# Filter stage of a graph kernel: 252 of 416 groups stored in source-block order and summed by matmuls

## The reference

```
h = relu(layernorm(x))
x = x + segment_sum(h[dst] * (softplus_shifted(edge_attr @ W1 + b1) @ W2 + b2), src)   # filter
h = relu(layernorm(x))
x = x + rgcn(relu(rgcn(h)))       # two relational convolutions, mean per (node, edge type)
```

## Time and profile before

| | us |
|---|---|
| median of 3 runs | 7748.82 (7742.09 to 7757.07) |
| the profiled execution | 7740.94, its span 7739.2 |
| busy: POOL / PE / DVE / ACT | 5938.5 / 4879.2 / 3524.5 / 3186.8 |
| chain that ended last | POOL 19%, all of it `got` at L1321 |
| GB/s moved, mean | 86 |

### The profile page before, as it was taken

One profiled execution on the slowest core, in us unless ns is written; L12 is line 12 of the kernel. 1 busy time (PEld: TensorE's weight loads), 2 busy tenths in 40 slices (PEclk: granted clock), 3 DMA queues, 4 the chain that ended last, 5 costly groups with the idle time before them and its releaser, 6 DMA issues. The chain is left out here.

```text
span 7739.2 us, 134678 instructions
## 1 busy us (share of the span) xinstructions
PE 4879.2 (63%) x27214; PEld 3639.4 (47%) x27214; DVE 3524.5 (46%) x10829; ACT 3186.8 (41%) x8459; POOL 5938.5 (77%) x5311
## 2 busy tenths in 40 slices
PE   1877777777777777686666666666644444444444
PEld 1656655665555556544444444444433333333333
DVE  6555555555555555486555555555521111111111
ACT  5555555555555555474333333333322222222222
POOL 4888888888888888846777777777767777777777
PEclk9988888888888888896666666666655555555555
DMA  8555555555555555584222222222222222222222
GB/s 262 86 84 84 84 84 84 84 83 84 84 84 84 84 84 84 70 304 134 70 80 80 78 79 80 77 80 80 77 61 56 56 56 56 56 56 56 56 56 54
DMA packets 587140, 663.53 MB, mean 86 GB/s; under 512 B 109683, under 2 KB 448091, under 8 KB 586755
## 3 DMA queue, kind: packets, MB, share of 16 engines
q0 software_dynamic: 352384, 340.33, 27.3%
q1 hardware_dynamic: 228934, 314.99, 12.9%
q10 hardware_dynamic: 5746, 7.42, 0.4%
HBM read 406.44 MB, written 255.87 MB: 86 GB/s over the span
## 5 line engine op out<-in xcount | busy, mean ns | idle before, releaser
L1321 POOL DMA_INDIRECT got<-table_dram,cidx x3328 | 3150.6, 947 | 1056.0 <-issue 1003.3
L980 POOL DMA_INDIRECT acc_dram<-total,idx x1664 | 2600.2, 1563 | 563.9 <-issue 361.1
L1369 PE MATMUL bank<-got,share 128*128 128x128 f32 x6656 | 1604.4, 417 | 1529.0 <-DMA got<-table_dram,cidx 1493.1
L1369 PEld LDWEIGHTS bank<-got,share 128*128 128x128 f32 x6656 | 1379.0, 307 | 1808.5 <-issue 1702.2
L1423 ACT ACTIVATE share<-cto_node,etcol 128x128 f32<-128x128 bf16 x3328 | 1082.5, 396 | 2756.3 <-PE bank L1369 1863.3
L240 DVE SCALAR_TENSOR_TENSOR xs<-bank,mask_hi,xs 128x128 f32 x416 | 146.0, 351 | 1681.6 <-PE bank L1369 1681.6
L946 DVE TENSOR_TENSOR msg<-bank,factor 128x512 f32<-128x512 f32 x416 | 287.8, 692 | 1219.1 <-issue 889.7
L871 ACT ACTIVATE total<-bank 128x258 f32<-128x258 f32 x832 | 275.5, 384 | 1200.4 <-DMA acc_dram<-total,idx 1200.4
L814 PEld LDWEIGHTS bank<-w,soft 128*128 128x128 f32 x3328 | 569.0, 242 | 33.1
L805 PE MATMUL bank<-msg,same 128*128 128x129 f32 x3328 | 583.9, 328 | 0.7 <-issue 0.7
L797 PE MATMUL bank<-rows,coef 2*128 2x512 bf16 x416 | 170.7, 410 | 653.1 <-DVE same L953 652.7
(11 more groups left out here) (178 smaller groups left out, 7667.1 us busy)
## 6 DMA issues: line engine op xcount, KB each, us to landing
edges<-in_edge_attr SPq DMA_DIRECT2D x415, 256.0 KB
got<-table_dram,cidx POOLq DMA_INDIRECT x3328
table_dram<-made SPq DMA_DIRECT2D x98, 512.0 KB, 3.7
table_dram<-umade SPq DMA_DIRECT2D x98, 512.0 KB, 2.9
win<-split_dram SPq DMA_DIRECT2D x416, 96.0 KB
acc_dram<-total,idx POOLq DMA_INDIRECT x1664, 3.3
acc_dram<-zeros SPq DMA_DIRECT2D x132, 192.0 KB, 2.8
sums<-acc_dram SPq DMA_DIRECT2D x196, 64.0 KB, 3.2
```

Source lines behind the costliest of these rows:

```text
L980: pool.indirect_dma_start(g.acc_dram[j][:, :], bass.IndirectOffsetOnAxis(ap=idx[k][:, j:j + 1], axis=0), total[k][:, j, 0:F], None, comput ...
L1321: pool.indirect_dma_start(got[k][:, j, :], None, g.table_dram[which][:, :], bass.IndirectOffsetOnAxis(ap=idx[k][:, j:j + 1], axis=0)).then ...
L1369: ins = nc.tensor.matmul(window[k], share[k][:, j, :], got[ka][:, j, :], start=j == 0, stop=j == TG - 1)
```

## The change

The 416 groups of the filter are split. `NA` = 252 groups are "plain": POOL stores their messages, one row of 129 floats (128 features and the source id), to a list `msg_dram` in the order of source blocks, with an indirect DMA without accumulation. The remaining 164 groups are "adding" and scatter as before; beside them, from the tenth on, the list is read back in units of 256 rows, four units per group, 154 sets (616 units), and each unit is summed into its block of `xs` by one-hot matmuls.

- `prepare`: the zeros are no longer written here. DVE gets the sorting: the source block of each of the 1,008 plain columns, 16 slab pairs of one-hots (`count_slabs`) that PE multiplies to a histogram, its running sums, and the rows, blocks and offsets of all units. Only the `dst` ids are split and stored.
- Plain groups: no `same`, no L805, L871, L914; instead a rank per edge by 8 small matmuls and four DVE operations. SP writes the zeros of `acc_dram` beside the first 200 groups.
- Both parts: the id row comes by a broadcast DMA (`load_low`, 128 KB) instead of a matmul; softplus takes one DVE instruction instead of two; `apart_by` goes.
- Adding groups: `src` ids also come by a broadcast DMA (256 KB).
- Convolution 0: the id row by the same broadcast DMA; L1359 goes, and L1466 reads SBUF instead of PSUM.

```diff
+        fits = UNITS * (self.NG - UNIT_LAG) - self.NBX
+        self.NA = fits // (UNITS + 2) // UNROLL * UNROLL
@@ prepare, vector
+            def count_slabs(n0, n1):
+                for n in range(n0, min(n1, len(slabs))):
+                    c0, count = slabs[n]
+                    need(dve, s_counted, n - 1)
+                    for to, size, digit in ((one_hi[n % 2], DIG, digits[0]), (one_lo[n % 2], LOW, digits[1])):
+                        ins = v.tensor_tensor(to[:, 0:count * size].rearrange("p (c d) -> p c d", d=size),
+                                              g.iota_c[:, 0:size, 0].unsqueeze(1).to_broadcast([P, count, size]),
+                                              digit[:, c0:c0 + count].unsqueeze(2).to_broadcast([P, count, size]), ALU.is_equal)
+                    ins.then_inc(s_binned, 1)
@@ filter, sync
+            def load_low(s, k):
+                need(sp, s_hot, s.at(NE - 1))
+                sp.dma_start(low[k][:, :], g.rows_dram[bass.ds(s.at(0), 1), 1, :].rearrange("a e -> (a e)").partition_broadcast(P)).then_inc(s_rows[k], 16)
+            def clear(chunk, j):
+                sp.dma_start(g.acc_dram[j][bass.ds(chunk * g.CLEAR, g.CLEAR), :].rearrange("(p r) f -> p (r f)", p=P),
+                             so.zeros[:, :]).then_inc(so.s_cleared, 16)
+                    if windows.own and s.live(UNIT_LAG, NA + g.NSET, NA):
+                        k = b.slot(NU, UNIT_LAG)
+                        if isinstance(s.i, int) and s.c == NA + UNIT_LAG:
+                            for j in range(TG):
+                                sp.wait_ge(s_sc[j], NA * 16)
+                        need(sp, s_red, b.at(UNIT_LAG + NU - 1))
+                        for m in range(UNITS):
+                            row = sp.value_load(so.unit_row[0:1, bass.ds(b.at(UNIT_LAG) * UNITS + m, 1)], min_val=0, max_val=NA * GE - UNIT)
+                            sp.dma_start(unit[k][:, m, :, :].rearrange("p k f -> p (k f)"),
+                                         g.msg_dram[bass.ds(row, UNIT), :].rearrange("(p k) f -> p (k f)", p=P)).then_inc(s_unit[k], 16)
@@ filter, tensor: plain, then adding
+                    if s.live(3, NA - 1):
+                        need(pe, s_sel, s.at(3) * 2 + 1)
+                        for j in range(TG):
+                            nc.tensor.matmul(ranks, so.others[:, :], one_hot[s.slot(2, 3)][:, :, j], start=False, stop=True,
+                                                   skip_group_check=True)
+                    if s.live(2, NA):
+                        need(pe, s_one, s.at(2) + 1)
+                        for j in range(TG):
+                            ins = nc.tensor.matmul(ranks, so.earlier[:, :], one_hot[s.slot(2, 2)][:, :, j], start=False, stop=True,
+                                                   skip_group_check=True)
+                        ins.then_inc(s_rank, 1)
+                        for m in range(UNITS):
+                            for k in range(UNIT // P):
+                                ins = nc.tensor.matmul(reduced[m], unit_hot[b.slot(2, lag)][:, m, k, :], unit[b.slot(NU, lag)][:, m, k, 0:F],
+                                                       start=k == 0, stop=k == UNIT // P - 1)
@@ filter, vector: plain
+                    if s.live(2, NA):
+                        need(dve, s_rank, s.at(2) + 1)
+                        v.tensor_tensor(chosen[:, :, :], one_hot[s.slot(2, 2)][:, :, :],
+                                        ranks.unsqueeze(2).to_broadcast([P, NBX, TG]), ALU.mult).then_inc(s_sel, 1)
+                    if s.live(1, NA):
+                        v.tensor_tensor(one_hot[s.slot(2, 1)][:, :, :], g.iota_c[:, 0:NBX, :],
+                                        so.src_blk[:, bass.ds(s.at(1) * TG, TG)].unsqueeze(1).to_broadcast([P, NBX, TG]),
+                                        ALU.is_equal).then_inc(s_one, 1)
+                        v.tensor_reduce(place[:, :], chosen[:, :, :].rearrange("p c j -> p j c"), AX_X, ALU.add).then_inc(s_sel, 1)
@@ filter, vector: adding
+            def add_unit(b, m):
+                lag = UNIT_LAG + 3
+                if m == 0:
+                    need(dve, s_red, b.at(lag) + 1)
+                at = dve.value_load(so.unit_blk[0:1, bass.ds(b.at(lag) * UNITS + m, 1)], min_val=0, max_val=NBX - 1)
+                to = g.xs[:, bass.ds(at, 1), :].rearrange("p a f -> p (a f)")
+                need(dve, s_added, b.at(lag) * UNITS + m)
+                v.tensor_tensor(to, to, reduced[m], ALU.add).then_inc(s_added, 1)
+                        for m in range(UNITS):
+                            ins = v.scalar_tensor_tensor(unit_hot[b.slot(2, lag)][:, m, :, :],
+                                                         unit[b.slot(NU, lag)][:, m, :, F:F + 1].to_broadcast([P, UNIT // P, P]),
+                                                         so.unit_off[:, bass.ds(b.at(lag) * UNITS + m, 1)],
+                                                         so.iota_f[:, :].unsqueeze(1).to_broadcast([P, UNIT // P, P]),
+                                                         ALU.add, ALU.is_equal)
@@ filter, gpsimd: plain
+                        pool.indirect_dma_start(g.msg_dram[:, :], bass.IndirectOffsetOnAxis(ap=idx[k][:, j:j + 1], axis=0),
+                                                total[k][:, j, :], None).then_inc(s_sc[k], 16)
```

More of the change, by code:

```diff
@@ L587, in _ @@
             variance(1)
[L588 to L596 removed]
+            split_chunks(3, 4)
@@ new lines, in adding, with step @@
+            def adding(windows, start, peel):
+                def step(s):
+                    b = s.behind(start)
+                    if s.live(0, NG, start):
+                        turn_edges(s)
+                    if s.live(1, NG, start):
+                        first_layer(s, False)
+                    if s.live(2, NG, start) and not windows.own:
+                        need(pe, s_rows[s.slot(NE, 2)], s.use(NE, 2) * 16 + 16)
+                        need(pe, s_hot, windows.number(s.at(2)))
+                        nc.tensor.matmul(bank_r[:, :], g.coef[0:2, :], rows[s.slot(NE, 2)][0:2, :],
@@ new lines, in add_unit, with adding, step @@
+            def add_unit(b, m):
[6 more added lines that the diff above has]
+                v.tensor_tensor(to, to, reduced[m], ALU.add).then_inc(s_added, 1)
+            def adding(windows, start, peel):
+                def step(s):
+                    b = s.behind(start)
+                    ready = windows.own and s.live(UNIT_LAG + 3, NA + g.NSET, NA)
+                    if ready:
+                        add_unit(b, 0)
+                    if s.live(2, NG, start):
@@ L911, in step @@
+                    if s.live(4, NG, start):
                         k = s.slot(NTO, 4)
@@ new lines, in adding, with step @@
+            def adding(start):
+                pool.wait_ge(so.s_cleared, 16 * TG * g.NCLEAR)
+                def step(s):
+                    k = s.slot(NTO, 0)
+                    need(pool, s_idx, s.at(0) + 1)
+                    for j in range(TG):
+                        need(pool, s_sc[j], s.at(0) * 16)
+                        apart(pool, g.gate)
+                        pool.indirect_dma_start(g.acc_dram[j][:, :], bass.IndirectOffsetOnAxis(ap=idx[k][:, j:j + 1], axis=0),
+                                                total[k][:, j, 0:F], None, compute_op=ALU.add).then_inc(s_sc[j], 16)
+                run_span(pool, start, NG, 0, step)
@@ L984, in _, with own_program @@
+            def own_program():
+                plain()
+                adding(NA)
+            if_own(pool, g, own_program, lambda: adding(0))
             for j in range(TG):
```

1006 lines of the change are left out of this document (669 added, 337 removed).

## The result

The changed kernel takes **7303.9 us** (median of 4 runs, 7301.7 to 7305.4) against 7746.7 us before (4 runs beside it): the ratio is 0.9426, with a 95% interval of 0.941 to 0.9443. The profiled execution took 7305.4 us with a span of 7303.7, so the two spans differ by 435.5 us.

A forecast was written before the change was run, and what follows sets the result against it. POOL's indirect DMAs were taken to bound filter and convolutions. From 7740.9 us, -597 (plain groups), +189 (adding groups), +8 (prepare), +12 (seam), +4 (convolution 0) and 8 to the median gave 7365 us, range 7160 to 7620.

The forecast's parts named there:

- Term 1: Plain groups: with a plain store at 0.95 us, 252 groups fall from 7.47 to 5.10 us each, -597 us.
- Rival A: Plain groups: the indirect store costs the accumulating one's 1.563 us, so slower than before, 7962 us; chance 0.12.
- rival D: Plain groups: DVE bounds them at 5.9 us per group, 202 us more, 7567 us; chance 0.13.
- Term 2: Adding groups: SP's issues take 8.7 us against POOL's 7.47 in 154 groups, +189 us.
- Term 3: Prepare: DVE's added sorting, less removed work and its waits for ACT, +8 us, bounds -15 and +40.
- Terms 4 and 5: Seam between plain and adding groups: pipeline drains and refills, +12 us; convolution 0: more bytes, POOL the bound, +4 us.
- Rival E: Convolution 0: DVE's comparison blocks POOL in each group, 141 us more, 7506 us; chance 0.03.
- B: Adding groups: the unit work is hidden, so term 2 is zero, 7176 us; chance 0.14.
- C: Adding groups: DVE's register loads lie bare or DMA is full, 10.3 us, 246 more, 7611 us; chance 0.13.

The follow-up runs named there:

- the accumulating variant: Changed kernel with the plain groups' stores accumulating into a list zeroed once; 9359.6 us on a second chip, where the kernel before takes 8889 us.
- Both edits together: Changed kernel without the unit register loads on SP and DVE: 7226.3 us; DVE's alone gone 7304.0 us, SP's alone gone 7241.6 us.
- the doubled blocks: Changed kernel with each of the 16 one-hot blocks of the prepare stage made twice by DVE: 7340.0 us.

## Why the prediction was right, and where it was off

**Term 1, plain groups: right.** Predicted 5.10 us per group and -597, measured 5.127 and -590. The 0.95 us for an operation that no row of before showed came from packet counts; the store takes 0.978 us and makes 32 packets (12438 for 390 of them in 1000 to 1500 us), and the accumulating variant brings 1.55 us and 112 more packets back. Rival A's condition thus fell as argued. DVE works 1055.6 / 252 = 4.19 us per plain group, where I had 4.6 to 5.0: rival D was further off than I gave it.

**Term 2, adding groups: right in mechanism, its size off by 67 us.** SP's chain was named as the first bound, and taking load off it is what gained. But my 8.7 us a step took 1.44 us for each of five register-addressed transfers from a single sequence of the earlier trace rows; the step above shows 1.20 us (source ids to window), 1.28 (window to first unit) and three times 1.17, then 0.54, 0.53 and 0.66 for the others: 7.72 us. The load proper, 0.438 us of the 1.44, has a median of 0.270 us at the window's line of the changed kernel; why, no run shows. The mis-sized prices make 154 x 0.98 = 151 us too much, five transfers 1.2 us too dear per group and three 0.2 too cheap. What came in its place is 0.54 us, or 84 us in all, by which a group with units lies above SP's 7.72: without the ten that have none and take 7.47, the mean is (164 x 8.213 - 10 x 7.47) / 154 = 8.26. The prediction treated SP and DVE as rivals of which the longer one counts, and left POOL at 7.47. In 1700 to 2600 us a group takes 900 / 108.5 = 8.29 us; POOL's own part of it is 7.7 and 0.58 is waiting for DVE's index, SP's is 7.7 to 7.9 and 0.38 is waiting for DVE's `same`, which frees the buffer of the source ids. So three engines of nearly the same length wait for one another. Both edits together gain 78 us where one alone gains 0 and the other 62; how the 0.54 us divide among the engines is argued from these waits and no run shows it. DVE's work was 714.9 / 108.5 = 6.6 us per group instead of 5.9: `same` at 1.08 instead of 0.68 us and the unit one-hots at 0.48 instead of 0.40 make the 0.7.

The estimate of the DMA load, 119 engine-us per group, met the trace: 0.92 x 16 x 900 / 108.5 = 122.

**Term 3, prepare: +19 instead of +8.** The work was sized right: DVE is busy 148.6 us up to 185 us against 106.0 up to 166 before, +42.6 for a forecast of 47 - 5. The waits were not: I had let all 33.8 us of the earlier trace rows go with the zeros, and of them 11.9 us stayed.

```profile
DVE rest L655 <- ACT split L544: 11.9, 5, 6.2
...
ACT split L544 <- DMA split_dram<-split: 58.1, 18, 6.2
```

ACT still waits for its stores, 58.1 us now against 30.2 before, although the DMA share of the stage fell from 0.91 to 0.41; taking the zeros away didn't speed the stores' return. That the doubled blocks moved the first scatter one for one shows DVE as the bound of the stage; why the stores return late wasn't tried.

**Terms 4 and 5: right.** Seam +10 for 12, tail +4 for 4. Convolution 0 has POOL's mean at 947 ns and 1565 us of work in 2090, as before, with a comparison that now reads SBUF:

```profile
L1959 DVE TENSOR_SCALAR cto_edge<-clow,part 128x512 bf16<-128x512 bf16 x375 | 137.5, 367 | 0.0
```

Rival E is refuted: 367 ns of it in every group, and the gathers don't stretch. The port rule of the Trainium skill (SBUF — State Buffer, Who interferes with whom) would have made it block POOL if the comparison runs in a two-port mode. This trace shows no blocking, and no row of it tells the mode. In the adding groups POOL's scatter did stretch, from 1577 without unit work to 1647 ns with it, 0.28 us per group. With half the unit bytes the mean was still 1644 ns, with three units 1589, without DVE's register loads 1624, so it isn't the bytes; whether DVE's instructions or the transfers stretch it, no run here tells apart.

**Rivals B and C.** B (all hidden, 7176) would have needed the period at 7.47; even without unit work it is 7.54, and beside it POOL's own work comes to 7.7. C's bare loads exist, at 0.24 us rather than 0.88.

The 61 us between forecast and result are term 2's -67, term 3's +11 and term 1's +7, the seam's -2, and some 10 because the changed kernel's median lies at its profiled run instead of 8 above it.

## To carry to other kernels

Price a queue's sequencer like an engine: a transfer whose address was loaded into a register first took 1.2 us of the issuing engine here, others 0.55, and spreading such transfers over two issuing engines gained as much as making their addresses constant. When engines have nearly the same length of work and wait for one another's buffers, expect the period above the longest of them (8.26 us here, over 7.72), and before relieving one, work out how near the next one is: here POOL's 7.7 us allowed 0.5 us per group at most. An indirect store with rows that are combined later can beat an indirect accumulation (0.96 against 1.55 us for 128 rows), if the combining fits beside it; packet counts of the queues pointed to the price before the operation was ever run.

## What the runs showed of the hardware

- Accumulating made an indirect DMA of 128 rows 0.6 us dearer on POOL and gave it 144 packets instead of 32, at equal bytes.
- A comparison of 128x512 that read its ids from SBUF with a step of four elements took 1.08 us, int32 or float32; with the ids in PSUM it took 0.68, and so did an add of two unstepped SBUF tiles of that size.
- A register load cost SP's sequencer 0.63 us per transfer, though the load proper took 0.27; on DVE, with work queued, 0.24 us stayed bare.
- Chips differed by more than the change is worth: one of them ran the kernel before 15% slower at the same instruction durations, and the kernel with three units, which ran on both kinds, 25% slower.
